# Query products of two tiles at once in a fused attention and expert kernel

## The reference

```
q = rmsnorm(x @ w_qa, q_norm_w) @ w_qb            # 192 latents, 16 heads of 128 + 64
kv = x @ w_kva                                    # 64 latents and 64 rope columns
kv_c, k_rope = kv[..., :64], kv[..., 64:]
k_nope, v = split(rmsnorm(kv_c, kv_norm_w) @ w_kvb)
q_rope, k_rope = rope(q_rope), rope(k_rope)
attn = softmax(causal(q @ k * scale))             # per head
x = x + (attn @ v) @ w_o
```

## Time and profile before

| | |
|---|---|
| median of 3 runs | 1339.07 us (1338.11 to 1340.1) |
| profiled execution, its time | 1338.7 us |
| its span | 1336.9 us |
| TensorE matmuls busy | 1231.2 us, 92% |
| VectorE busy | 813.2 us, 61% |
| ScalarE busy | 454.2 us, 34% |
| GpSimd busy | 378.8 us, 28% |
| scores of group 0 start | 58.78 us |

### The profile page before, as it was taken

The page is one execution under the profiler, slowest core; times in us unless marked ns, Lnnn a source line. Parts: engine busy times, 40 slices in busy tenths (PEclk is TensorE's granted clock), DMA queues, the critical chain, the costliest instruction groups (busy, mean ns, idle before and its releaser), DMA issues.

```text
span 1336.9 us, 19470 instructions
## 1 busy us (share of the span) xinstructions
PE 1231.2 (92%) x6004; PEld 760.4 (57%) x6004; DVE 813.2 (61%) x2238; ACT 454.2 (34%) x1041; POOL 378.8 (28%) x464
## 2 busy tenths in 40 slices
PE   6999999999999899998989999997578899899988
PEld 3566566555655556556556777775235446465454
DVE  6367767787578966785533333334576776676431
ACT  2455525453445425452201111110232533424311
POOL 1243013362425412362250000115364271510200
PEclk9799999999999999999999999998679899999999
DMA  9999999999900100011348888983111011100000
GB/s 317 413 420 420 420 421 419 420 419 417 420 35 28 68 1 1 1 52 44 101 129 256 259 266 273 285 260 118 48 55 48 24 52 36 37 12 17 0 16 16
DMA packets 89422, 235.48 MB, mean 176 GB/s; under 512 B 12769, under 2 KB 23681, under 8 KB 89089
## 3 DMA queue, kind: packets, MB, share of 16 engines
q1 hardware_dynamic: 70912, 192.54, 38.9%
q0 software_dynamic: 9216, 25.18, 5.9%
q10 hardware_dynamic: 9216, 16.78, 3.3%
HBM read 66.70 MB, written 167.77 MB: 175 GB/s over the span
## 4 chain that ended last, share of the span: by engine, by line
PE 69%; DVE 23%; issue 4%; POOL 2%; ACT 1%; DMA 1%; SPq 1%; ACTq 0%; POOLq 0%; DVEq 0%
PE bank L1329 5%; PE bank L529 5%; PE bank L617 4%; PE bank L488 4%; PE bank L1309 4%; PE bank L489 4%; PE bank L555 4%; DVE negmax L861 4%; PE bank L1582 3%; DVE r L872 3%; PE bank L1571 3%; PE bank L1565 3%; PE bank L538 3%; PE bank L1335 3%; PE bank L1294 2%
## 5 line engine op out<-in xcount | busy, mean ns | idle before, releaser
L708 ACT ACTIVATE r<-bank,negmax 128x128 f32<-128x128 f32 (+3 forms) x256 | 135.2, 528 | 174.3 <-DVE negmax L861 173.8
L529 PE MATMUL bank<-r 128*128 128x512 f32 (+3 forms) x512 | 184.3, 443 | 0.0
L861 DVE TENSOR_REDUCE negmax<-bank 128x1 f32<-128x128 f32 (+3 forms) x256 | 124.5, 487 | 44.6 <-PE bank L530 41.6
L972 POOL TENSOR_TENSOR r<-r,tables 128x256 f32<-128x256 f32 x56 | 42.0, 749 | 330.5 <-ACT r L689 330.3
L538 PE MATMUL bank<-tables,r 128*128 128x128 f32 x640 | 115.0, 278 | 12.2 <-DVE r L872 11.6
L1196 POOL DMA_INDIRECT sent<-r,slots x96 | 93.9, 978 | 99.8 <-DVE slots L1117 40.1
L1411 DVE COPY r<-bank 128x512 f32<-128x512 f32 x64 | 41.2, 686 | 120.5 <-PE bank L1335 76.2
L538 PEld LDWEIGHTS bank<-tables,r 128*128 128x128 f32 x640 | 72.7, 141 | 65.9 <-DVE r L872 31.4
L872 DVE TENSOR_SCALAR r<-r,rrow 128x128 f32<-128x128 f32 (+3 forms) x256 | 104.5, 408 | 0.3
L529 PEld LDWEIGHTS bank<-r 128*128 128x128 f32 x512 | 77.8, 191 | 23.6 <-issue 18.3
L1210 POOL DMA_INDIRECT r<-sent,slots x20 | 21.7, 1085 | 219.1 <-DVEq L1409 212.8
(11 more groups left out here) (266 smaller groups left out, 2390.5 us busy)
## 6 DMA issues: line engine op xcount, KB each, us to landing
sent<-gath SPq DMA_DIRECT2D x8, 16384.0 KB, 94.3
r<-waT_dram SPq DMA_DIRECT2D x64, 304.0 KB, 3.4
r<-sent SPq DMA_DIRECT2D x64, 256.0 KB, 3.4
sent<-r ACTq DMA_DIRECT2D x64, 256.0 KB, 4.1
w2buf<-wcT_dram SPq DMA_DIRECT2D x64, 48.0 KB, 3.5
r<-w_o_dram SPq DMA_DIRECT2D x1, 2048.0 KB, 11.0
sent<-gath SPq DMA_DIRECT2D x2, 1024.0 KB, 57.0
out_dram<-x SPq DMA_DIRECT2D x4, 512.0 KB, 2.9
```

What stands on the lines that cost most here:

```text
L529: nc.tensor.matmul(at[:, 0:n], QT[g % 2][:, h, i * P:(i + 1) * P], KT[:, 0:n], start=True, stop=False)
L708: nc.scalar.activation(prob[:, u % 4, 0:(i + 1) * P], bank[SCORE[u % 4]][:, 0:(i + 1) * P], ACT.Exp, bias=negmax[:, u:u + 1], scale=1.0, a ...
L861: nc.vector.tensor_reduce(negmax[:, u:u + 1], bank[SCORE[u % 4]][:, 0:(i + 1) * P], axis=AX.X, op=ALU.max, negate=True).then_inc(A["max"], 1)
```

## The change

A product step now makes two tiles. The first 128 latents of both tiles are multiplied in four matmuls of 256 columns, two heads each, into halves of banks 7 and 6. The further 64 latents stand twice, in rows 0 to 63 and 64 to 127 of `cq2`; `wqe2` holds the weights of heads 0 and 1 of a group in the lower rows and those of heads 2 and 3 in the upper, so that four matmuls of 64 rows follow, alternating between the two halves of rows and the two banks. ScalarE copies each bank for both tiles. Products stand at slots 6 and 8 (1 and 3 in head group 0), turns at 10, 12, 13 and 15 (unchanged in head group 0). The normalization's halves move to slots 5 and 7, their copies to 6 and 8. The counts move to slot 2 and into bank 7, the work on them to VectorE's slots 3 to 10, and the wait for them from the values to the products. POOL makes its first 8 sends ahead of the ropes instead of between them. The two clearings of zero rows fall away, and a third instruction in `latents` writes the second copy of the further latents.

```diff
-        wqe2, e = carve(r2, e, (HEADS, QE))
+        wqe2, _ = carve(r2, e, (HEADS // 2, QE))
+        e += HEADS * QE
...
-                last = nc.tensor.matmul(bank[6 + h // 8][0:QL2, c:c + KVL], wqbT[:, h, P:QL], wkvT[:, 0, h, :],
+                r, c = QL2 * (h // 2 % 2), (h // 4 * 2 + h % 2) * KVL
+                last = nc.tensor.matmul(bank[6][r:r + QL2, c:c + KVL], wqbT[:, h, P:QL], wkvT[:, 0, h, :],
...
-            for m in range(2):
-                for dst, b, n in ((wqe1, 4, P), (wqe2[0:QL2], 6, QL2)):
-                    nc.scalar.copy(dst[:, 8 * m:8 * m + 8, 0:KVL],
-                                   bank[b + m][0:n, :].rearrange("p (h c) -> p h c", h=8)).then_inc(prep_out, 1)
+            for dst, at in ((wqe1[:, 0:8], 4), (wqe1[:, 8:16], 5), (wqe2, 6)):
+                nc.scalar.copy(dst[:, :, 0:KVL], bank[at][:].rearrange("p (h c) -> p h c", h=8)).then_inc(prep_out, 1)
...
-        PRODUCT_AT = {1: 0, 3: 1, 5: 2, 7: 3}
-        TURN_AT = {9: 0, 11: 1, 13: 2, 15: 3}
+        Q_BANKS = (QUERY, VALUE)
+        PRODUCTS_AT = ({6: 0, 8: 1}, {1: 0, 3: 1})
+        TURN_AT = ({10: 0, 12: 1, 13: 2, 15: 3}, {9: 0, 11: 1, 13: 2, 15: 3})
...
-            def q_product(g, i, at):
+            def q_products(g, m):
+
                 hg = g % GROUPS
-                w1 = wqe1[:, hg * HG:(hg + 1) * HG, :].rearrange("p h c -> p (h c)")
-                w2 = wqe2[:, hg * HG:(hg + 1) * HG, :].rearrange("p h c -> p (h c)")
-                nc.tensor.matmul(bank[at][:], cq1[:, i * P:(i + 1) * P], w1, start=True, stop=False)
-                nc.tensor.matmul(bank[at][:], cq2[:, i * P:(i + 1) * P], w2, start=False, stop=True)\
-                    .then_inc(A["q"], 1)
+                two = 2 * QE
+                w2 = wqe2[:, 2 * hg:2 * hg + 2, :].rearrange("p h c -> p (h c)")
+                for t in range(2):
+                    for half in range(2):
+                        w1 = wqe1[:, hg * HG + 2 * half:hg * HG + 2 * half + 2, :].rearrange("p h c -> p (h c)")
+                        nc.tensor.matmul(bank[Q_BANKS[half]][:, t * two:(t + 1) * two], cq1[:, q_tile(2 * m + t)], w1,
+                                         start=(t == 0), stop=False)
+                for t in range(2):
+                    for half in range(2):
+                        r = slice(QL2 * half, QL2 * (half + 1))
+                        last = nc.tensor.matmul(bank[Q_BANKS[half]][:, t * two:(t + 1) * two], cq2[r, q_tile(2 * m + t)],
+                                                w2[r, :], start=False, stop=(t == 1))
+                        if t:
+                            last.then_inc(A["q"], 1)
...
-                pe.wait_ge(A["cq"], 2 * b + 2)
-                for i in range(TB):
-                    if i >= 2:
-                        pe.wait_ge(A["qs"], TB * g + i - 1)
-                    q_product(g, i, 7 - i % 2)
+                pe.wait_ge(A["cq"], 3 * b + 3)
+                q_products(g, 0)
+                pe.wait_ge(A["qs"], TB * g + 2)
+                q_products(g, 1)
...
-                if not final and with_next and at in PRODUCT_AT:
-                    i = PRODUCT_AT[at]
-                    if i == 0:
+                if not final and with_next and at in PRODUCTS_AT[first]:
+                    m = PRODUCTS_AT[first][at]
+                    if m == 0:
                         pe.wait_ge(A["qte"], TB * g + TB)
+                        need(pe, A["ote"], 3 * g)
+                        if g % GROUPS == 1:
+                            need(pe, R["ranked"], g // GROUPS)
                     else:
-                        pe.wait_ge(A["qs"], TB * (g + 1) + i)
-                    q_product(g + 1, i, QUERY)
+                        pe.wait_ge(A["qs"], TB * (g + 1) + 2)
+                    q_products(g + 1, m)
...
-                    if at == 3:
-                        pe.wait_ge(A["qte"], TB * (g + 1))
+                    if at == 5:
+                        pe.wait_ge(A["qs"], TB * (g + 1) + TB)
                         norm_tensor(pe, N1, c, xn1, 0)
-                    if at == 6:
+                    if at == 7:
...
-                if g % GROUPS == 1 and at == 7:
-                    pe.wait_ge(A["ote"], 3 * g)
-                    route_counts(pe, c, 6)
+                if g % GROUPS == 1 and at == 2:
+                    pe.wait_ge(A["qte"], TB * (g + 1))
+                    route_counts(pe, c, QUERY)
...
+            def q_copies(g, m):
+                two = 2 * QE
+                for half in range(2):
+                    act.wait_ge(A["q"], TB * g + 2 * m + half + 1)
+                    nc.scalar.copy(qs[:, 2 * m:2 * m + 2, half * two:(half + 1) * two],
+                                   bank[Q_BANKS[half]][:].rearrange("p (t c) -> p t c", t=2)).then_inc(A["qs"], 1)
...
-                    nc.vector.scalar_tensor_tensor(out=cq2[0:QL2, :], in0=bank[1][0:QL2, :], scalar=qn2[:],
-                                                   in1=rq[0:QL2, :], op0=ALU.mult, op1=ALU.mult)\
-                        .then_inc(A["cq"], 1)
+                    for half in range(2):
+                        nc.vector.scalar_tensor_tensor(out=cq2[QL2 * half:QL2 * (half + 1), :], in0=bank[1][0:QL2, :],
+                                                       scalar=qn2[:], in1=rq[0:QL2, :], op0=ALU.mult, op1=ALU.mult)\
+                            .then_inc(A["cq"], 1)
...
-                pool.wait_ge(A["qs"], TB * g + i + 1)
+                pool.wait_ge(A["qs"], TB * g + 2 * (i // 2) + 2)
...
+                    if b and hg == GROUPS - 1:
+                        send_ready(pool, b - 1)
+                        for n_sent in range(2 * TB):
+                            send(b - 1, n_sent)
```

80 lines of the change are left out of this document (35 added, 45 removed).

## The result

| | kernel before | changed kernel |
|---|---|---|
| median | 1338.59 us (1337.73 to 1340.1, 4 runs) | 1350.75 us (1349.56 to 1354.83, 4 runs) |
| span of the profiled execution | 1336.9 us | 1349.1 us |
| first scores to last scores | 551.6 us | 562.05 us |
| from the last scores to the end | 726.5 us | 728.5 us |

The ratio is 1.0102 [1.0088, 1.0115]: slower, by 12.2 us. The forecast was 1334.9 us, the range ended at 1342.5 us. So the sign and most of the size are settled.

A forecast was written before the change was run, and what follows sets the result against it. The prediction took TensorE as the bound, with VectorE close behind where routing rides along. Its terms summed to -4.2 us, from 1338.7 to 1334.5 us, a median of 1334.9 us; the range was 1329 to 1342.5 us.

The forecast's parts named there:

- preparation of batch 0: Preparation before batch 0's attention: one copy less, -0.3 us.
- first products, batches 1 to 3: Between batches: the second pair waits for both copies, the rope starts later, scores start 1.7 us later; +5.1 us in all.
- third latent instruction: VectorE's queue ahead of the key latent's transposes: 0.7 us more a batch, 0.4 us hidden by slack; +1.0 us over three batches.
- head group 0: Products at slots 1 and 3: normalization and logits wait for copies, +1.1 us in batches 1 to 3, -0.5 in batch 0; +2.8 us.
- head groups 1 and 2 of batch 0: Products at slots 6 and 8: gain 1.2 us, bare slots cost 0.64 us; -0.55 us a group, -1.1 us.
- head group 1 of batches 1 to 3: Product of slot 6 waits 0.9 us for the counts, but waits of slots 11 and 15 go, 1.3 us; -3.9 us in all.
- head group 2 of batches 1 to 3: VectorE enters slot 9 with nothing left over; slots 9 to 15 take 11.5 us instead of 13.2; -7.8 us in all.
- head group 3, slots 0 to 14: Head group 3 has no products, so no change was expected.
- after the attention: From the last scores to the end: the prediction named no term, counted as 0 us.
- The pair of tiles: Query products: half-row matmuls run side by side, two tiles take 2.95 us instead of 3.54, a gain of 0.6 us.
- rival (a): Turns' waits stay in groups 5, 6 and their like, as ScalarE's copy stands behind an exponential: 1345 us, slower; chance 0.17.
- rival (b): Ropes hold up VectorE, 0.6 us a collision, one more in each of six groups, 3.6 us: 1338.5 us, no change; chance 0.23.

The follow-up runs named there:

- `e7_sends_between`: Changed kernel with the eight sends of a batch put back between the ropes of head group 2, two behind each: 1356.19 us, ratio 1.0119.
- `e2_turn_copy_first`: Changed kernel with ScalarE's copy of a turned tile ahead of the exponential of the same slot instead of behind it: 1393.73 us on a slower chip, ratio 1.0146.
- `e10_three_mends`: Changed kernel with turn and normalization copies ahead of their slot's exponential, and own banks for the second first pair in batches 1 to 3: 1337.33 us, ratio 0.9982.
- `e13_mends_and_weigh`: `e10_three_mends` plus, in head group 2, VectorE's portions in slot 5, two weighings in slot 6 and one in slot 14: 1339.14 us, ratio 0.9977.
- experiments 8 and 9: Changed kernel with the third turn in slot 14 (1359.3 us, 1.0137); or products in 5 and 7, turns in 9, 11, 13, 15 where possible (1356.71 us, 1.0135).
- `e9_products_5_7`: Changed kernel with products in slots 5 and 7, turns in 9, 11, 13 and 15 where no counts stand in their bank: 1356.71 us, ratio 1.0135.
- `e6_weigh_early`: Changed kernel with head group 2's portions in slot 5 instead of 8, weighings in slots 6, 8, 14 instead of 10, 12, 14: 1349.95 us, ratio 1.0074.
- `e4_own_banks`: Changed kernel with the second pair of first products of batches 1 to 3 in banks 5 and 4: 1394.26 us on a slower chip, ratio 1.0151.
- `e5_after_alone`: Changed kernel without any edit, run again on a third chip: 1351.3 us, ratio 1.0079 to the kernel before.
- experiments 5 to 14 and 16: Changed kernel unedited, and variants of it with copies, banks, weighings, sends, turns, products or the third latent instruction moved: 1332.05 to 1359.3 us.
- `e1_full_rows`: Changed kernel with the further 64 latents multiplied over all 128 rows, the upper ones zero: 1405.44 us on a slower chip, ratio 1.0234.

## Why the prediction was wrong

Term by term, from the first scores' starts of both traces:

| term of the sum | predicted us | measured us, changed less before |
|---|---|---|
| preparation of batch 0 | -0.3 | -0.2 |
| first products, batches 1 to 3 | +5.1 | +6.1 |
| third latent instruction | +1.0 | +1.65 |
| head group 0 | +2.8 | +4.5 |
| head groups 1 and 2 of batch 0 | -1.1 | -0.65 |
| head group 1 of batches 1 to 3 | -3.9 | +1.4 |
| head group 2 of batches 1 to 3 | -7.8 | -1.4 |
| head group 3, slots 0 to 14 | 0 | -1.15 |
| after the attention | 0 | +2.0 |
| sum | -4.2 | +12.2 |

The terms for head group 2 that the prediction states, 2.8 and twice 2.4 us, make 7.6 us and not 7.8; that slip of 0.2 us changes nothing here.

**Right.** The pair of tiles (2.94 us), shown by undoing it. The place and kind of the waits at the first products, at the normalization (0.97 us), the logits (15.74 us), and 0.92 us on L1109's work (L1095 in the kernel before) before the first product of group 5. Moving the sends ahead of the ropes is no loss: undone, it costs 6.6 us in groups 6, 10 and 14 (`e7_sends_between`).

**The failed step: "slots 9 to 15 take 11.5 us instead of 13.2 us, about TensorE's own time", and in head group 1 "then saves the waits of slots 11 and 15".** The walks up to slot 9 were right: 18.3 us in group 5 (forecast 18.0) and 16.35 us in group 6 (16.2). From there group 5 takes 13.2 us and group 6 13.5 us. The waits of slots 11 and 15 went, and others came at slots 12 and 13: 0.56 and 0.68 us, and 0.27 and 1.29 us. I had compared TensorE's 3.2 us between two turns with the length of a copy. The copy starts only after the exponential of its slot, so it is VectorE's queue that has to be followed to the end, through the densest stretch, and that I walked only up to slot 9. `e2_turn_copy_first` shows it: the same work with the copy ahead gives 1.4 us in groups 5, 9 and 13, and slots 9 to 15 of group 5 then take 11.6 us, near the 11.5 us of the forecast (29.5 less 18.0). In groups 6, 10 and 14 the order of the copies is half of it: `e10_three_mends` gave 1.35 us there and lost 1.28 us in the next group, and only with the weighings in slots 6 and 14 as well (`e13_mends_and_weigh`) were groups 6 and 7 together 1.05 us shorter than in the changed kernel (28.79 + 19.61 against 29.84 + 19.61). With the turns in other slots VectorE's delay showed before other turns (experiments 8 and 9). These two terms are 11.7 us off, 16.4 us being the whole error against the sum.

This is rival (a), with the collisions of rival (b) in it. I gave (a) 0.17. Its condition was that over two thirds of the waits stay; the waits at slots 12 and 13 are 1.24 us in group 5 and 1.56 us in group 6, 2.8 of its 3.3 us. Its picture was incomplete in one point: it spoke of turns that follow each other by one slot, and `e9_products_5_7` shows a wait of 1.12 us with two. How the loss divides between VectorE's own work and GpSimd's ropes beside it isn't settled. Moving the weighings under the products gave 0.34 us in group 6 (`e6_weigh_early`) and 1.0 us in groups 6 and 7 together (`e13_mends_and_weigh`), though the eight moved instructions met more of the ropes and took 4.1 and 3.5 us instead of 3.2. So these gains come of their place in VectorE's queue and not of fewer collisions. VectorE's normalizations met the ropes too: one took 0.95 us at 253.43 in group 5, against 0.45 us of its form. A kernel without ropes beside VectorE wasn't tried.

The Trainium skill, in "SBUF — State Buffer" under "SBUF: two separate sides", has VectorE and GpSimd exclude each other at a shared pair of ports for a whole instruction, when VectorE's has two inputs in SBUF or runs in a mode that takes two ports. The trace agrees in direction: L1147, with two such inputs of 128x64 elements, takes 0.28 us in the median and 0.81 us at most, the longest beside a rope.

**Sizes.** The first products were 5.6 us at the full clock, 1.85 us a batch (forecast 1.7), and 0.5 us more by the clock in batch 2. `e4_own_banks` shows 1.2 of the 1.85 us to be the wait for the copies. The third latent instruction cost 0.55 us a batch instead of 0.33. Counted from the start of slot 15 (158.13 before, 157.66 after) the key latent starts 0.88 us later (183.05 in the earlier trace rows, now 183.46), not 0.7, of which the slack hid 0.33, not 0.4. In head group 0, groups 4 and 12 grew by 0.9 and 1.2 us as forecast (1.1). Group 8 grew by 2.0 us, of which 0.8 us is clock: its window has a granted clock of 0.96, and in `e5_after_alone` it takes 27.88 us instead of 28.70. Group 0 grew by 0.4 us instead of shrinking by 0.5; `e2_turn_copy_first` takes 0.65 us off it, so the copy's place held it up too.

**Not shown to be the change's:** the 2.0 us after the attention. In the eleven further runs of the changed kernel and its variants on the other chips (experiments 5 to 14 and 16) that part took 726.8 to 731.0 us, and nothing was edited in it; in the two kernels with the old products 726.5 and 726.6 us. That the lowest are these two stays unexplained. The loss by the attention alone is 10.2 us up to the last scores.

## What to carry to other kernels

When a copy that frees a bank stands in a queue behind an instruction that waits for a third engine, count that engine's lateness and not only the copy's length; walk that engine's queue through the densest stretch to its end, not only to where the change acts. A matmul form that fills two banks at once also hands them over at once, so look at the order in its consumers' queues with it: here the attention was 10.5 us longer with the old order and 6.7 us shorter with copies first, banks of their own, the extra instruction off the path and the weighings moved. Give the kernel before every mend that isn't the change's own, or what the mend is worth is booked to the change. And a wait that goes is looked for in the following slots and groups before it is counted as a gain.

## What the runs showed of the hardware

- The pairs on half the rows run side by side: eight passes of 256 columns on 64 rows take 1.06 us to the next matmul, where eight over 128 rows take 1.73 us (`e1_full_rows`, 99.56 to 101.29).
- Chips differed more than the change did: the kernel before took 1372.12 us on one and 1338.59 to 1341.5 us on the others, with a granted clock of 0.958 in the median of its runs there and 0.967 on the others. In the windows of group 6 the granted clock was 0.95 in all four runs on the slower chip and 1.00 in every profiled execution on the others.
- Around the first products the clock dropped in some executions and not in others: the stretch had 0.88 to 0.97 in several kernels and 1.00 in others. The unchanged changed kernel had 0.96 in group 8 in one execution and 1.00 there in another (`e5_after_alone`), so it isn't set by the instructions alone.
- VectorE's and GpSimd's ropes take longer when they start together: on VectorE the eight ropes took 15.1 us in the kernel before and 21.1 us in the changed one, and GpSimd's first multiplication of 128x256 elements took 0.97 us at 193.12 instead of 0.72 us.
